# Lower halves of the narrow stages' turned inner tiles: ACT's f32 copy and POOL's subtraction, or one DVE instruction from PSUM

## The reference

```python
def fp4_quant_dequant(x):                      # blocks of 16 along the last dim
    xb = x.reshape(shape[:-1] + (shape[-1] // BLOCK, BLOCK))
    scale = jnp.maximum(jnp.max(jnp.abs(xb), axis=-1, keepdims=True) / 6.0, 1e-12)
    xn = xb / scale
    q = _GRID[jnp.searchsorted(_MID, jnp.abs(xn))] * jnp.sign(xn) * scale
    ...
def _L0_ffn_ref(x, w_gate, w_up, w_down):      # 256 -> 704 -> 256
    h = silu(fp4_linear(x, w_gate)) * fp4_linear(x, w_up)
    return fp4_linear(h, w_down)
...
x = x + 0.5 * _L0_ffn_ref(_layernorm(x, axis=-1), ...)
x = x + _L0_attn_ref(_layernorm(x, axis=-1), ...)
x = x + 0.5 * _L0_ffn_ref(_layernorm(x, axis=-1), ...)
x = x + 0.5 * _L1_ffn_ref(_layernorm(x, axis=-1), ...)
x = x + _L1_attn_ref(_layernorm(x, axis=-1), ...)
x = x + 0.5 * _L1_ffn_ref(_layernorm(x, axis=-1), ...)
```

## Time and profile before

| what | value |
|---|---|
| time, median of 3 runs | 2859.77 us (2859.61 to 2860.03) |
| the profiled execution's own time | 2863.14 us |
| its span | 2861.2 us |
| granted TensorE clock, mean | 0.942 of full speed |
| PE busy | 2420.5 us, 85% |
| DVE busy | 1953.1 us, 68% |
| ACT busy | 1687.1 us, 59% |
| POOL busy | 1074.0 us, 38% |

### The profile page before, as it was taken

One profiled execution on the slowest core, in us unless ns is written; L12 is line 12 of the kernel. 1 busy time (PEld: TensorE's weight loads), 2 busy tenths in 40 slices (PEclk: granted clock), 3 DMA queues, 4 the chain that ended last, 5 costly groups with the idle time before them and its releaser, 6 DMA issues.

```text
span 2861.2 us, 55968 instructions
## 1 busy us (share of the span) xinstructions
PE 2420.5 (85%) x23228; PEld 1837.5 (64%) x23228; DVE 1953.1 (68%) x3305; ACT 1687.1 (59%) x2898; POOL 1074.0 (38%) x823
## 2 busy tenths in 40 slices
PE   2777787877898988889898988899988888889888
PEld 1455555655676776667575766666765667767667
DVE  7688788988687876767678667678776772434432
ACT  2255566555767766566666565666664565547554
POOL 0144445543343533153535353444444352122112
PEclk9799999999999999999898989999998899999999
DMA  3100000000000000000000000000000000000000
GB/s 126 46 1 1 1 1 1 1 1 1 1 1 1 1 1 10 15 13 13 13 13 13 13 13 13 12 13 13 13 12 21 9 1 8 8 8 1 8 8 8
DMA packets 34843, 32.90 MB, mean 11 GB/s; under 512 B 7648, under 2 KB 33952, under 8 KB 34592
## 3 DMA queue, kind: packets, MB, share of 16 engines
q1 hardware_dynamic: 34592, 29.33, 3.1%
HBM read 12.28 MB, written 4.19 MB: 6 GB/s over the span
## 4 chain that ended last, share of the span: by engine, by line
PE 52%; DVE 25%; ACT 9%; POOL 6%; issue 6%; SPq 1%; DMA 1%; DVEq 0%; POOLq 0%; ACTq 0%
PE psum L625 13%; PE psum L627 12%; PE psum L626 12%; PE psum L631 4%; PE psum L1057 2%; PE psum L1059 2%; PE psum L1058 2%; DVE a1pr L1781 2%; POOL f1hT L2052 2%; POOL a1pr L2039 2%; PE psum L908 2%; DVE a1c L1799 1%; DVE f1e L1892 1%; PE psum L961 1%; DVE a1nm L1758 1%
## 5 line engine op out<-in xcount | busy, mean ns | idle before, releaser
L2052 POOL TENSOR_TENSOR f1hT<-f1g,f1hT 128x512 f16<-128x512 f32 x256 | 304.8, 1197 | 791.5 <-ACT f1hT L1447 791.0
L2039 POOL TENSOR_TENSOR a1pr<-a1PT,a1pr 128x1024 f16<-128x1024 f32 (+1 forms) x176 | 351.3, 1999 | 293.5 <-DVE a1pr L1781 293.5
L625 PE MATMUL psum<-f1sl,f1w1h 128*128 128x256 f16 x1024 | 287.8, 281 | 16.8 <-ACT f1g L1442 8.6
L625 PE MATMUL psum<-f1w2h,f1hT 128*128 128x256 f16 x1024 | 280.1, 273 | 11.5 <-POOL f1hT L2052 9.1
L626 PE MATMUL psum<-f1sl,f1w1h 128*128 128x256 f16 x1024 | 287.0, 280 | 0.0
L627 PE MATMUL psum<-f1sl,f1w1l 128*128 128x256 f16 x1024 | 286.7, 280 | 0.0
L627 PE MATMUL psum<-f1w2h,f1hT 128*128 128x256 f16 x1024 | 279.1, 273 | 0.0
L626 PE MATMUL psum<-f1w2l,f1hT 128*128 128x256 f16 x1024 | 279.1, 273 | 0.0
L1758 DVE TENSOR_REDUCE a1nm<-psum 128x2 f32<-128x768 f32 (+3 forms) x176 | 198.2, 1126 | 78.0 <-PE psum L888 77.2
L1781 DVE CAST a1pr<-a1PT 128x1024 f16<-128x1024 f32 (+1 forms) x176 | 156.2, 892 | 86.4 <-ACT a1PT L1343 67.1
L625 PE MATMUL psum<-wguh,f0xT 128*128 128x352 f16 x512 | 164.9, 322 | 42.7 <-DVE f0xT L1605 14.2
(11 more groups left out here) (336 smaller groups left out, 7434.9 us busy)
## 6 DMA issues: line engine op xcount, KB each, us to landing
a1Q<-a1st SPq DMA_DIRECT2D x96, 64.0 KB, 2.6
a1K<-a1st SPq DMA_DIRECT2D x96, 64.0 KB, 2.6
x<-in_L_attn_x SPq DMA_DIRECT2D x8, 512.0 KB, 8.8
out<-x SPq DMA_DIRECT2D x8, 512.0 KB, 2.9
wslot<-in_L_ffn_w SPq DMA_DIRECT2D x1, 1024.0 KB, 7.7
wraw<-in_L_ffn_w SPq DMA_DIRECT2D x1, 1024.0 KB, 5.6
wslot<-in_L_ffn_slot_embeds SPq DMA_DIRECT2D x1, 1024.0 KB, 7.8
a1Q<-a1mr SPq DMA_DIRECT2D x64, 4.0 KB, 1.7
```

The costliest lines, as they stand in the source:

```text
L625: e.matmul(out, lh, rh, start=start, stop=False)
L2039: e.tensor_tensor(a1["pr"][:, i % 2, 1, :, 0:w], a1["PT"][:, i % 2, :, 0:w], a1["pr"][:, i % 2, 0, :, 0:w], ALU.subtract).then_inc(s["a1_pl"])
L2052: e.tensor_tensor(hT1[:, 1, 2 * hp:2 * hp + 2, :], gg[:, hp % 2, :, :], hT1[:, 0, 2 * hp:2 * hp + 2, :], ALU.subtract).then_inc(s["f1_hl"])
```

## The change

The f32 copy of ACT and the subtraction of POOL go. DVE makes the lower half in one instruction: it reads the bank in PSUM, multiplies by HS and subtracts the upper half that ACT wrote. The bank is released, and the down matmuls start, by that DVE instruction (f0_hl). ACT's remaining copy raises a semaphore with a new name, f0_hh. The first use of `f0Y` two tiles later waits for POOL's product (f0_hq) of the earlier tile in place of the subtraction.

```diff
-                        banks.after(2 + p, "f0_hY", 2 * ft + p + 1)
+                        banks.after(2 + p, "f0_hl", 2 * ft + p + 1)
...
-                        src = psum[:, 2 + p, 0:n]
-                        e.activation(f0["hT"][:, t % 2, 0, cs], src, ACT.Copy, scale=HS)
-                        e.activation(f0["Y"][:, t % 2, cs], src, ACT.Copy, scale=HS).then_inc(s["f0_hY"])
+                        e.activation(f0["hT"][:, t % 2, 0, cs], psum[:, 2 + p, 0:n], ACT.Copy, scale=HS).then_inc(s["f0_hh"])
...
-                    q.wait_ge("f0_hl", 2 * (ft - 1))
+                    q.wait_ge("f0_hq", ft - 1)
                     e.tensor_reduce(c_, blocks16(h), AX, ALU.max, apply_absolute_value=True).then_inc(s["dve"])
...
+            def f0_halves(f):
+                S = at_f0(f)
+                for t in range(NT):
+                    ft = 4 * f + t
+                    G = S + 10.0 + 10.0 * t
+                    for p in range(2):
+                        cs = slice(4 * P * p, 4 * P * p + (4 * P, 2 * P)[p])
+                        yield G + 16.0 + 1.2 * p
+                        q.wait_ge("f0_hh", 2 * ft + p + 1)
+                        hT = f0["hT"][:, t % 2, :, cs]
+                        e.scalar_tensor_tensor(hT[:, 1, :], psum[:, 2 + p, 0:cs.stop - cs.start], HS, hT[:, 0, :],
+                                               ALU.mult, ALU.subtract).then_inc(s["f0_hl"])
...
-            def f0_halves(f):
...
-                        yield G + 16.5 + 1.2 * p
-                        q.wait_ge("f0_hY", 2 * ft + p + 1)
-                        e.tensor_tensor(f0["hT"][:, t % 2, 1, cs], f0["Y"][:, t % 2, cs], f0["hT"][:, t % 2, 0, cs],
-                                        ALU.subtract).then_inc(s["f0_hl"])
```

More of the change, by code:

```diff
@@ L1947, in vector @@
             return [weights(), weight_halves(), straight(), slot_weights(), a1_constants(),
-                  *[chain(z, 2 * B) for z in (f0_tokens, f0_hidden, f0_update)],
+                  *[chain(z, 2 * B) for z in (f0_tokens, f0_hidden, f0_halves, f0_update)],
                   *[chain(z, B) for z in (a0_front, a0_blocks, a0_update, a1_front, a1_max, a1_probs, a1_ctx)],
@@ L2053, in f1_mlp @@
                                         ALU.subtract).then_inc(s["f1_hl"])
-            return [weights(), *[chain(z, 2 * B) for z in (f0_powers, f0_products, f0_hidden, f0_halves)],
+            return [weights(), *[chain(z, 2 * B) for z in (f0_powers, f0_products, f0_hidden)],
                   *[chain(z, B) for z in (a0_powers, a0_values, a1_powers, a1_probs)],
```

## The result

| what | before | after |
|---|---|---|
| time, median | 2859.9 us (2859.6 to 2862.1) | 2812.0 us (2809.2 to 2815.2) |
| span of the profiled execution | 2861.2 us | 2813.3 us |
| DVE busy | 1953.1 us | 1990.1 us |
| ACT busy | 1687.1 us | 1643.1 us |
| POOL busy | 1074.0 us | 948.4 us |

What follows compares the result with a forecast made beforehand. DVE (84% busy) was taken to bound stage 1 and PE (90%) stage 2. The terms 13.6 + 4.9 - 7.1 - 2 - 3.4 + 4.6 made +10.6 us: 2870 us from a median of 2859.8, range 2845 to 2894.

Steps and rivals of the forecast that it cites:

- Part 3: DVE's net load charged at 0.84 in stage 1 (110 to 690 us), 0.37 in stage 2 (690 to 1116): +13.6, +4.9 us.
- Part 6: Banks 2 and 3 released 0.5 us later by DVE; 15 PE waits in stage 1, at 0.61: +4.6 us.
- rival D: Later stages, reordered by the planner: +-7 us of either sign; no chance of its own, widens the other cases.
- Part 1: Two added DVE instructions per f0 tile, 0.94 us: 35.7 us in stage 1, 23.5 us in stage 2.
- Part 2: DVE instructions stretch less without POOL's subtraction: 19.5 us back in stage 1, 10.2 us in stage 2.
- Rival C: DVE's queue sets all of stage 1: +44 us, 2904 us, three quarters of it 2893; chance 0.15.
- Part 4: ACT loses its f32 copies, 47 us in stages 1 and 2, at 0.15 of the chain: -7.1 us.
- Part 5: POOL loses 128 subtractions: -2 us of DVE's waits, -3.4 us of PE's waits for a0v.
- Part 7: Waits that move, including the shorter hop to the down matmuls: nothing of its own.
- Rival A: DVE has slack enough in stage 1, net load charged at 0.37: -1.6 us, some 2858 us; chance 0.20.
- Rival B: DVE waits for ACT, so removed copies count in full: -32 us, half of it 2844 us; chance 0.23.
- its marks: Rival B's signs: stage 1 shorter than 580 us, DVE's waits for ACT there shrinking from 47 us by half.

Runs made afterwards that it cites:

- e1: New work issued in the engine orders planned for the kernel before, DVE's instruction inserted at the planned time of ACT's copy: 2875.1 us, ratio 1.0049.
- e14: Kernel after in its own order without DVE's lower half; ACT's copy releases the bank and starts the down matmuls, output incomplete: 2800.5 us.
- e2: Old work (two ACT copies, POOL's subtraction) issued in the order planned for the kernel after: 2844.9 us, ratio 0.9937.
- e6: Kernel after in its own order, plus a POOL subtraction of constants as load after ACT's copy: 2838.0 us.
- e5: Kernel after in its own order, plus ACT copies of constants of the removed sizes, as load alone: 2823.5 us.
- e3: Kernel before, same work; planner's assumed delay of a signal from DVE 140 instead of 120 ns, so another order: 2847.7 us, ratio 0.9940.
- e9: Kernel after, same work; planner's assumed delay of a signal from POOL 130 instead of 110 ns, so another order: 2834.2 us, ratio 0.9903.
- e13: Kernel after in its own order, plus a DVE reduction of constants behind each new DVE instruction, nobody waiting for it: 2842.7 us.
- e7: Kernel after in its own order, new DVE instruction made twice (the second dose), the second one releasing the bank: 2847.1 us.

## Why the prediction was wrong

**In short.** The prediction took all its rows from the order of before and carried their prices over to a kernel that the planner orders anew. For the order of before its sum was near, though not by each of its terms: e1, the new work in that order, is 15.1 us slower by the medians, and +10.6 had been forecast. In the order that was issued two steps failed: the charge for DVE's load and the bank's release (parts 3 and 6, 43.3 us, measured 12 to 19), and rival D, which left the order of f0's own stages at nothing and gave the later ones 7 us (measured 33).

**What bounds the kernel** was read rightly as far as it went: in stage 1 DVE is the busiest engine, after the change more so. What did not follow is that work added to it pushes the end back by its busy share.

**Part 1, DVE's added time**: right. 684 and 414 ns against 0.68 and 0.42, and with the order held DVE is busy 898.4 us up to f0's end in the kernel after and 839.3 in e14: 59.1 us, where 35.7 + 23.5 = 59.2 had been said.

**Part 2, what DVE gets back**: right. With the order held, DVE's busy time up to f0's end is 867.1 us with the old work (e2) and 898.4 with the new, +31.3 us where +29.5 had been said, so 59.1 - 31.3 = 27.8 us came back against 29.7. POOL's subtraction alone gives 19.9 of them (e6). Between the kernels before and after, whose orders differ, the rise is smaller, 486.2 to 497.2 us in the first stage and 310.4 to 322.7 in the second. a0a's mean fell from 736 to 665 ns, not below 650, and a0Sr's, of the same list, rose from 751 to 847 ns; the sum is better than its single entries. The rule of the Trainium skill on the shared port ("SBUF — State Buffer", section "SBUF: two separate sides") agrees again: a0a has 753 and 749 ns with POOL's subtraction back, and the new instruction, from PSUM with one SBUF operand, has 680 to 686 in every kernel.

**Part 3, the charge for DVE's load, is the step that failed.** It took 0.84, DVE's busy share, in stage 1. In gross terms the prediction charged DVE's added time with 0.84 x 35.7 + 0.37 x 23.5 = 38.7 us, and part 6 another 4.6: 43.3 us for what e14 measures at 18.5 by f0's end and at 11.5 by the medians. Over 59.2 us of added time that is 0.2 to 0.3 per busy microsecond, under the 0.37 of the chain of waits, which the prediction had at hand and used for stage 2 alone. Solid rows of DVE and 91% in a stretch of 100 us had spoken for the higher charge, and its sign, DVE at 85% or more in stage 1, came true with 87%; neither shows that PE has no other work to put in meanwhile. PE did: with 29.3 us of waits for the new instruction, it was still busy 461 of 570 us. Rival C rested on the same step and fell with it. It is not out of the world: the second dose costs 35 us by the medians, 0.6 per microsecond. Nor was the charge wrong in every order. If ACT's and POOL's shares cost in the order of before what they cost in that of after, some 36 us together, then DVE's costs about 15.1 + 36 = 51 us there, more than the 43.3; that is an estimate, no run has it alone.

**Part 4, ACT**: right, 8.5 to 11.5 us measured (e5) against 7.1. **Part 5 with the relief of part 2, POOL**: right, 26.0 to 27.8 us measured (e6) against 20.2 + 5.4 = 25.6. **Part 6, the later release**, was a wait of the order of before. There it was put too low: e1's gate matmuls wait 32.0 us for the bank, 23.2 more than before and not 7.5, since 24 of them wait where 15 did and only those 15 had been counted. In the order of after it is all but gone, 1 us. **Part 7** had put the shorter hand-off, one engine in place of two, at nothing. In the order of after, the old work ends f0 29.5 us later; 27.8 + 8.5 - 18.5 = 17.8 of these are the three loads, and 11.7 are left (6.9 by the medians). The hand-off is a candidate, but the down matmuls wait as long for DVE's half as for POOL's (28.3 and 29.1 us), no run had it alone, and the prices need not add up.

With 18.5 in place of 43.3 the sum is 18.5 - 25.6 - 7.1 = -14.2 us, and f0's end moved by -14.6. That they agree so closely is luck, since the order had its own part in it (+14.9 with the old work), and 11.5 could be put in with as much right as 18.5.

**The second failure is rival D's size.** It was named and placed rightly: the stretch after the last edited instruction changed its length with no edit in it, and the order did that. It was priced at 72 matmuls x 0.10 us = 7 us; the count was right (3558 against 3487 in the last stretch), the price was not. The stretch is 28.2 us shorter: PE is busy 16.9 us less, some 9 of it for the 71 matmuls (437.03 / 3558 = 0.123 us each) and most of the other 8, by estimate, with the granted clock, 0.97 against 0.95, and is idle 11.3 us less (57.3 against 68.7). Where it is idle differs altogether. The waits of PE in the last stretch, before and then after:

```profile
PE psum L1057 <- DVE f1d L1888: 14.7, 6, 2.9
PE psum L631 <- ACT f1u L1424: 9.4, 6, 1.7
```

```profile
PE psum L625 <- ACT f1g L1440: 20.4, 10, 3.6
PE psum L625 <- DVE f1pr L1946: 11.8, 11, 1.4
```

Which exchange of rows does it stays open. The number of matmuls left over is a hint at most: e3, with the old work, has 3494 of them and the same 476.7 us, but e9 has 3448 and 490.1 us.

D was kept to the later stages. In f0's own the order matters as much: it alone moves f0's end by 31 us with the old work and by 28 us with the new, and it decides at which matmuls PE waits.

**Rival A** (DVE has slack, 2858 us) had the charge that comes nearer in the order of after; with D's widening it reached 2851. **Rival B** (2844 us) would have been affirmed by its marks, or nearly: stage 1 is shorter than 580 us, and DVE's nine recurring waits for ACT fell from 47 to 27 us. Yet its reason fell: with ACT's time given back the kernel is 8.5 to 11.5 us slower, where B needed 37. Those waits shrank with the whole stage, and what ends a wait is not what it costs. Stage 2 kept its 426 us within 5 (421.5), and DVE's new instructions stayed below 0.75 us, both as said. **The rule against the change**, that some work may better leave a saturated DVE for Scalar or GPSIMD (the Trainium skill, "Perfetto Trace Analysis", section "Optimizing Scalar/DVE Operations"), pointed the wrong way for orders planned with the new work: at 84% busy, DVE did better by taking over what cost ACT and POOL some 36 us. In the order of before it pointed the right way: e1 is 15.1 us slower.

Without the luck of the draw the sum would still have been wrong for a kernel that is planned anew. Over the orders measured the work gains 30.5 us, and the forecast said +10.6.

## What to carry to other kernels

A busy share is no price. Here added work on an engine that is busy 84% cost 0.2 to 0.3 per microsecond in an order planned for it, about 0.6 with a second dose, and by estimate over 0.8 in an order that had the bank's next user waiting. Ask which matmul waits and for what, the bank or the operand, before and after; a sum over releasers mixes the two. Work removed from a half idle engine can be dear, as POOL's was, with its instructions ahead of another operand and DVE's busy time stretched beside them. Where a planner orders everything anew, prices read in the old order need not hold: compare works over several orders each, or hold the order still. Here the order alone moved the same work by up to 46 us, more than the 30 us of the edit. And read a price from several executions, not from one profile.

## What the runs showed of the hardware

- With the order of after held, ACT's 128 copies cost 8.5 to 11.5 us and POOL's 128 subtractions 26.0 to 27.8 us, though ACT is busy 58% and POOL 34% of the span in the kernel after. POOL's stretch DVE's other instructions by 19.9 us (e6).
- An added DVE instruction that reads PSUM and one SBUF operand has a mean of 680 to 686 ns at 512 columns, with POOL's subtraction beside it (e6) or without, and one over an SBUF operand alone 674 ns (e13); a0a, with two SBUF operands, has a mean between 555 and 753 ns in the kernels that hold the order of after, and is fastest where DVE has most to do (555 in e13, 586 in e7).
- The granted clock of the last stretch, 0.94 to 0.95 in the order of before and 0.97 in that of after, goes with the order and not with the edited work.
